# Edge sums of a graph kernel: a 16-column one-hot per tile as stationary operand, in partition quarters, placed by a second product

## What is computed

```python
e   = relu(bn(edge_attr @ ee_w1 + ee_b1, ee_g1, ee_bb1)) @ ee_w2 + ee_b2     # 212500 x 16 -> 128
h   = x + segment_sum(e, dst, N)
z   = h + segment_sum(h[src], dst, N)
z   = relu(bn(z @ mlp_w1 + mlp_b1, ...)); z = relu(bn(z @ mlp_w2 + mlp_b2, ...))
out = layernorm(x + z)
```

## Time and profile before

| | |
|---|---|
| median of three runs | 2196.79 us |
| profiled execution | 2194.66 us |
| its span | 2192.5 us |
| granted TensorE clock, mean over the span | 0.978 |
| PE, DVE, POOL, ACT busy, share of the span | 95%, 78%, 73%, 48% |

### The profile page before, as it was taken

One profiled execution on the slowest core, in us unless ns is written; L12 is line 12 of the kernel. 1 busy time (PEld: TensorE's weight loads), 2 busy tenths in 40 slices (PEclk: granted clock), 3 DMA queues, 4 the chain that ended last, 5 costly groups with the idle time before them and its releaser, 6 DMA issues. The chain is left out here.

```text
span 2192.5 us, 53444 instructions
## 1 busy us (share of the span) xinstructions
PE 2086.0 (95%) x16230; PEld 1694.0 (77%) x16230; DVE 1707.0 (78%) x2494; ACT 1051.6 (48%) x1986; POOL 1601.1 (73%) x1595
## 2 busy tenths in 40 slices
PE   6699999999984999999999999999999999999977
PEld 6699999999952777777777777777777777777637
DVE  5399999999997777777777777777777777777566
ACT  0022222222244555555555555555555555555576
POOL 3288888888868777777777777777777777777405
PEclk8799999999996999999999999999999999999999
DMA  9433333333343211111111111111111111111106
GB/s 212 132 106 105 105 103 104 102 104 104 105 151 126 54 54 53 53 53 53 53 53 53 53 53 53 53 53 53 53 53 53 53 53 53 52 53 54 32 25 210
DMA packets 108752, 169.88 MB, mean 77 GB/s; under 512 B 36800, under 2 KB 65104, under 8 KB 108666
## 3 DMA queue, kind: packets, MB, share of 16 engines
q1 hardware_dynamic: 69213, 96.46, 15.3%
q0 software_dynamic: 34944, 71.64, 11.8%
q10 hardware_dynamic: 4561, 1.36, 0.3%
HBM read 156.54 MB, written 12.81 MB: 77 GB/s over the span
## 5 line engine op out<-in xcount | busy, mean ns | idle before, releaser
L814 POOL DMA_INDIRECT table<-h_scratch,idx x1092 | 1031.1, 944 | 338.0 <-issue 320.9
L946 DVE TENSOR_TENSOR table<-ps,keys 128x880 bf16<-128x880 f32 (+1 forms) x780 | 777.4, 997 | 204.9 <-PE ps L836 193.9
L836 PE MATMUL ps<-table 128*128 128x220 bf16 x2860 | 527.8, 259 | 23.8 <-DVE table L946 23.7
L902 ACT CAST counts_even<-ps 128x440 bf16<-128x440 f32 (+1 forms) x780 | 397.7, 510 | 312.5 <-PE ps L836 291.4
L849 PE MATMUL ps<-table,counts_even 128*128 128x384 bf16 x2600 | 541.7, 326 | 0.0
L849 PE MATMUL ps<-table 128*128 128x384 bf16 x2600 | 538.8, 325 | 0.0
L902 ACT CAST table<-ps 128x440 bf16<-128x440 f32 (+1 forms) x780 | 388.1, 498 | 286.2 <-PE ps L836 261.5
L836 PEld LDWEIGHTS ps<-table 128*128 128x128 bf16 x2860 | 282.7, 101 | 184.0 <-DVE table L946 25.0
L587 PE MATMUL ps<-table 128*128 128x96 f32 x3328 | 415.6, 278 | 0.0
L587 PEld LDWEIGHTS ps<-table 128*128 128x128 f32 x3328 | 389.6, 193 | 0.0
L529 ACT ACTIVATE table<-table,low_rows_sb 128x512 fp32r<-128x512 f32 x208 | 145.0, 720 | 385.4 <-DMA table<-in_edges_t 364.5
(11 more groups left out here) (156 smaller groups left out, 1267.8 us busy)
## 6 DMA issues: line engine op xcount, KB each, us to landing
table<-in_edges_t SPq DMA_DIRECT2D x416, 128.0 KB, 2.5
table<-h_scratch,idx POOLq DMA_INDIRECT x1092, 2.5
table<-in_edges SPq DMA_DIRECT2D x26, 512.0 KB, 7.1
table<-in_x_t SPq DMA_DIRECT2D x48, 256.0 KB, 3.1
h_scratch<-table SPq DMA_DIRECT2D x24, 256.0 KB, 2.2
out<-table SPq DMA_DIRECT2D x24, 256.0 KB, 2.9
table<-in_dst_mixed SPq DMA_DIRECT2D x1, 832.0 KB
table<-in_dst_tiles SPq DMA_DIRECT2D x1, 832.0 KB, 12.5
```

What stands on the lines that cost most here:

```text
L814: pool.indirect_dma_start(near_rows[:, t, :], None, h_dram, bass.IndirectOffsetOnAxis(ap=idx[:, v, t:t + 1], axis=0)).then_inc(gathered[u] ...
L836: mm = pe.matmul(ps[:, LIST_BANKS[p % RING], (t % 2) * LIST_COLS:(t % 2 + 1) * LIST_COLS], low_match[:, v, t, :], match[:, t, :], start=Tr ...
L902: act.copy(counts[(v * LISTS + c) % 2][:, :, 2 * k * NARROW:(2 * k + tiles) * NARROW].rearrange("p b (t w) -> p b t w", t=tiles), ps[:, LI ...
L946: dve.tensor_tensor(match[:, first:last, :], ps[:, 0, 0:LIST_COLS].unsqueeze(1).broadcast_to([P, last - first, LIST_COLS]), keys[:, v, c, ...
```

## The change

The one-hot of a tile becomes 16 columns wide, counted from the first node of that tile (`tile_base`), and is now the stationary operand. The moving operand is the 128 rectified features of the tile with a column of ones behind them (129 columns), so that sums and count come out of one f32 product per tile. Tiles 0 to 3 of a group write the PSUM partition quarters 0 to 3 (16 rows in each), tiles 4 to 7 the same quarters beside them. A second product then puts these rows at their nodes: DVE makes `group_placing`, a one-hot of 2 times 96 columns per group (`place_groups`), ACT copies the sums and the counts out of PSUM (`keep_sums`), and PE multiplies them (`fold_tiles`: two bf16 and two f32 products of 96 columns). `halve` and the counts' four products fall away, and so does the copy of the node numbers in PSUM: `make_onehot` and `place_groups` read `iota` in SBUF. `add_window` comes one group later.

The condition for a single round now also asks that each tile spans under 16 nodes.

```diff
         def window_sums(dve):
-            nodes = ps[:, 5, 0:WINDOW]
+            nodes = iota[:, 0:SLIM]
             def make_onehot(g, u):
                 wait(dve, sums_done, g - 1)
-                dve.tensor_tensor(onehot[:, u % 2], nodes... [P, GROUP_TILES, WINDOW], rel..., ALU.is_equal)
+                dve.tensor_tensor(slim_onehot[:, u % 2], nodes... [P, GROUP_TILES, SLIM], rel..., ALU.is_equal)
             def clamp(g, u):
...
-                dve.tensor_tensor(rows[:, u % 2, :].rearrange("p (t d) -> p t d", d=D),
+                dve.tensor_tensor(edge_rows[:, u % 2, :, 0:D],
...
+            def place_groups(g, u):
+                wait(dve, folded, g - 1)
+                dve.tensor_tensor(group_placing[:, u % 2],
+                                  iota.unsqueeze(1).broadcast_to([P, GROUP_SETS, WINDOW]),
+                                  group_place[:, bass.ds(g * GROUP_SETS, GROUP_SETS)].unsqueeze(2)
+                                  .broadcast_to([P, GROUP_SETS, WINDOW]), ALU.is_equal).then_inc(placed, 1)
...
                         make_onehot(i * BODY + u + 1, u + 1)
                         clamp(i * BODY + u + 1, u + 1)
-                    add_window(i * BODY + u, u)
+                    place_groups(i * BODY + u, u)
+                    if not (first and u == 0):
+                        add_window(i * BODY + u - 1, u - 1)
...
                 @block.scalar
+                    def keep_sums(g, u):
+                        act.wait_ge(sums_done, g + 1)
+                        wait(act, folded, g - 1)
+                        act.copy(tile_counts[:, u % 2], sums_bank(u)[:, :, D:].broadcast_to([P, GROUP_SETS, P]))
+                        act.copy(tile_sums[:, u % 2], sums_bank(u)[:, :, 0:D]).then_inc(sums_kept, 1)
+                    def body(i, last=False):
                         for u in range(BODY):
-                            high(i, u)
+                            if u < 2:
+                                high(i, u + 2)
+                            elif not last:
+                                high(i + 1, u - 2)
+                            keep_sums(i * BODY + u, u)
...
                 @block.gpsimd
-                            halve(i, u)
...
                 @block.tensor
                     def sums(g, u):
-                        wait(pe, added, g - 1)
+                        wait(pe, sums_kept, g - 1)
                         pe.wait_ge(onehot_done, g + 1)
-                        pe.wait_ge(halved, g + 1)
-                        for t in range(GROUP_TILES // 2):
-                            pe.matmul(ps[:, 4 + 2 * (u % 2), WINDOW:2 * WINDOW], ones_bf[:], halves[:, u % 2, t, :], ...)
                         pe.wait_ge(clamped, g + 1)
                         for t in range(GROUP_TILES):
-                            mm = pe.matmul(ps[:, 4 + 2 * (u % 2), 0:WINDOW], rows[:, u % 2, t * D:(t + 1) * D],
-                                           onehot[:, u % 2, t, :], start=(t == 0), stop=(t == GROUP_TILES - 1))
+                            q = t % QUARTERS
+                            mm = pe.matmul(sums_bank(u)[32 * q:32 * q + SLIM, t // QUARTERS, :], slim_onehot[:, u % 2, t, :],
+                                           edge_rows[:, u % 2, t, :], start=True, stop=True, tile_position=(0, 32 * q))
                         mm.then_inc(sums_done, 1)
+                    def fold_tiles(g, u):
+                        wait(pe, added, g - 1)
+                        pe.wait_ge(sums_kept, g + 1)
+                        pe.wait_ge(placed, g + 1)
+                        for k in range(GROUP_SETS):
+                            pe.matmul(folded_at(u)[:, 1, :], tile_counts[:, u % 2, k, :],
+                                      group_placing[:, u % 2, k, :].bitcast(BF16)[:, 1:2 * WINDOW:2], ...)
+                        for k in range(GROUP_SETS):
+                            mm = pe.matmul(folded_at(u)[:, 0, :], tile_sums[:, u % 2, k, :], group_placing[:, u % 2, k, :], ...)
+                        mm.then_inc(folded, 1)
...
                                 features(g + 1, u + 1)
                             sums(g, u)
+                            if not (first and u == 0):
+                                fold_tiles(g - 1, u - 1)
```

More of the change, by code:

```diff
@@ L37 @@
 WINDOW = 96
+SLIM = 16
+QUARTERS = 4
 NEAR = 64
@@ L125, in build @@
         block_mask = carve(0, P)
-        dst_i = carve(0, ALL_TILES).bitcast(I32)
+        tile_base = carve(0, ALL_TILES)
+        dst_i = tile_base.bitcast(I32)
+        group_place = carve(0, GROUPS * GROUP_SETS)
         ones = carve(0, P)
@@ L171, in build @@
         prod = sb("prod", [ED, 2, D])
[L172 to L175, removed]
+        least = sb("least", [MIXED, ROW_ENDS])
+        most = sb("most", [MIXED, ROW_ENDS])
+        turned_ends = sb("turned_ends", [MIXED, QUARTERS, MIXED_TILES // QUARTERS])
         base = sb("base", [P, BASES])
@@ L267, in _ @@
-                act.wait_ge(base_out, 16 * (4 + DENSE))
+                                  least[:, GATHER_AT[-1] + t:GATHER_AT[-1] + t + 1]).then_inc(base_out, 16)
+                act.wait_ge(base_out, 16 * (6 + DENSE))
                 act.dma_start(base[:], base_dram.rearrange("(o g) -> o g", o=1).broadcast_to([P, BASES])
                               ).then_inc(base_in, 16)
-                act.wait_ge(ones_set, 2)
+                act.wait_ge(ones_set, 3)
+                for q in range(QUARTERS):
+                    act.dma_start(group_place[32 * q:32 * q + SLIM, :],
+                                  quarters_dram[q:q + 1, :].broadcast_to([SLIM, GROUPS * GROUP_SETS])).then_inc(place_in, 16)
@@ L339, in _ @@
                 mixed = table[0:MIXED, 1, 0:MIXED_EDGES].bitcast(I32)
[L340 to L345, removed]
+                for k, (op, far) in enumerate(((ALU.min, least), (ALU.max, most))):
+                    dve.tensor_reduce(far[:, 0:MIXED_TILES], mixed.rearrange("r (t e) -> r t e", e=P), AX_X, op
                                       ).then_inc(ends, 1)
                     dve.wait_ge(ends, k + 1)
-                    dve.tensor_reduce(far[:, STREAMS + DENSE:], far[:, STREAMS:STREAMS + DENSE], AX_X, op
+                    at = MIXED_TILES
+                    dve.tensor_reduce(far[:, at:at + ROW_GROUPS],
+                                      far[:, 0:MIXED_TILES].rearrange("r (j t) -> r j t", j=ROW_GROUPS), AX_X, op)
+                    at += ROW_GROUPS
+                    for j in range(STREAMS):
+                        dve.tensor_reduce(far[:, at + j:at + j + 1], far[:, GATHER_AT[j]:GATHER_AT[j + 1]], AX_X, op)
+                    at += STREAMS
+                    if k == 0:
+                        dve.tensor_copy(turned_ends[:], far[:, 0:MIXED_TILES].rearrange("r (i q) -> r q i", q=QUARTERS))
+                    dve.tensor_reduce(far[:, at:at + 1], far[:, GATHER_AT[-1]:MIXED_TILES], AX_X, op
                                       ).then_inc(base_ready, 1)
@@ L491, in body @@
                         clamp(i * BODY + u + 1, u + 1)
-                    add_window(i * BODY + u, u)
+                    place_groups(i * BODY + u, u)
+                    if not (first and u == 0):
+                        add_window(i * BODY + u - 1, u - 1)
+            dve.memset(edge_rows[:, :, :, D:], 1.0)
+            for u in range(2):
+                dve.memset(sums_bank(u), 0.0)
             make_onehot(0, 0)
             clamp(0, 0)
-            body(0)
+            body(0, first=True)
             with dve.Fori(1, BODIES - 1) as i:
@@ L530, in high @@
                                        ACT.Copy, scale=low_rows[:, 0:1]).then_inc(high_done, 1)
-                    for u in range(BODY):
-                        high(0, u)
-                    with act.Fori(1, BODIES) as i:
-                        for u in range(BODY):
-                            high(i, u)
+                    def keep_sums(g, u):
[4 more added lines that the diff above has]
+                    def body(i, last=False):
+                        for u in range(BODY):
+                            if u < 2:
[3 more added lines that the diff above has]
+                            keep_sums(i * BODY + u, u)
+                    high(0, 0)
+                    high(0, 1)
+                    body(0)
+                    with act.Fori(1, BODIES - 1) as i:
+                        body(i)
+                    body(BODIES - 1, last=True)
                 @block.gpsimd
```

134 lines of the change are left out of this document (77 added, 57 removed).

## The result

The changed kernel takes 2221.88 us (median of four runs, 2218.34 to 2224.34) against 2197.28 for the kernel before, a ratio of 1.0111 with a 95% interval of 1.0093 to 1.0128: 1.1% slower, clear of no change. The profiled execution took 2218.34 us with a span of 2216.5, so the comparison with the profile before is +24.0 us of span.

The account below looks back on a forecast made before the run. PE was full before; with the change, DVE and POOL blocking at SBUF was to bound. 208 x (2.8 - 2.528) = +56.6, +4, +1 on 2194.66, runs 2.1 above: 2258 us, range 2130 to 2343, the case's own 2217 to 2311.

Parts of the forecast that it names:

- the period of 2.8 us: Edge stage: time per group with the change, taken at 2.8 us against 2.528 before, +56.6 us over 208 groups.
- DVE's own sum: Edge stage: DVE's work per group, 2.05 us against 2.52 before, including 0.16 of issue behind add_window.
- PE's sums: Edge stage: 16 instructions of 129 moving columns per group, taken at 1.0 us between bounds of 0.45 and 1.79.
- the period of 2.7 to 3.0: Edge stage: sign of being right, 2.7 to 3.0 us per group with PE idle before sums and fold_tiles.
- The blocking term: Edge stage: DVE operations with two SBUF inputs and POOL's split wait for each other, at least 0.6 us per group.
- the two orders of `split` and the placing operation: Edge stage: placing operation first gives 2.73 us per group, split first gives 2.99.
- the prediction's own formula: Edge stage, split first: period P is 2.05 + (2.7 - P + 1.28) - 0.06, so 2.99 us.
- The cost of the change of width: PE running empty between full width and quarters, twice per group: 0 to 0.28 us each, taken at 0.15.
- Prologue and tail: Added DVE operations and later Gram loads before the edge stage, +4 us; one more keep_sums, fold_tiles and addition after, +1.
- Rival 2: Edge stage: f32 products on quarters don't overlap, PE bounds at 3.2 us per group, 2341 us; chance 14%.
- rival 1: Edge stage: split falls under the clamp, so the kernel is faster, 2176 us, other end 2123; chance 30%.
- Rival 3: Edge stage: four quarters fully side by side, sums at 0.45 us, 2239 us if SBUF waits hold; chance 15%.

Follow-up runs that it names:

- Experiments 1 and 2: Kernel before, make_onehot reading iota in SBUF: 2329.81 us. Changed kernel, node numbers in PSUM for both operations, only placing, only one-hot: 2103.98, 2103.57, 2104.05 us.
- both_psum: Changed kernel with make_onehot and place_groups reading node numbers from PSUM and the placed sums sharing one bank: 2103.98 us, ratio 0.9566.
- one_fold_bank: Changed kernel with the placed sums in one PSUM bank instead of two, all node numbers still in SBUF: 2222.28 us, ratio 1.0107.
- pad_act: Changed kernel with one more ACT copy of 256 elements per group, its result unused: 2246.81, 2248.93, 2250.66 and 2131.14 us.
- place_psum: Changed kernel with only place_groups reading node numbers from PSUM and the placed sums sharing one bank: 2103.57 us, one run at 2172.6.
- place_first: Changed kernel with the placing operation ahead of the clamp on DVE: 2195.43 us, ratio 0.9981.
- experiment 3: The run one_fold_bank: changed kernel with the placed sums in one PSUM bank instead of two, 2222.28 us.
- experiment 7: ACT's high one group earlier, ahead of keep_sums: on both_psum 2072.42 us, on the changed kernel 2222.34 us.

## Why the prediction came out as it did

The direction and the mechanism were right, the size was not: +61 us forecast, +24.6 measured. The step that failed is the period of 2.8 us, for which 2.614 was measured: 208 x 0.186 is the 39 us too much. Its two terms that were mis-sized are DVE's own sum and PE's sums. The time lies in the stated range of 2217 to 2311, near its lower end, but the period of 2.7 to 3.0, named as a sign of being right, did not come.

- **The blocking term was right in kind.** The prediction asked for a placing operation or one-hot far above 0.3 us. It is 1.043. The sum of the three means is 0.33 + 1.04 + 1.28, 0.73 above 0.29 + 0.355 + 1.28, where at least 0.6 was named. Experiments 1 and 2 show the cause.
- **The period was taken at 2.8 and is 2.61.** It was chosen between 2.73 and 2.99, the two orders of `split` and the placing operation, and both were too long. *DVE's sum of 2.05*: I counted in every group the 0.16 of issue that the earlier trace rows show behind one `add_window`. In the trace before, only 49 of 206 groups have it, all of them groups in which DVE had just waited for PE. The last groups of the stage have no `split` beside them and show DVE's own pace, 645.25 - 643.39 = 1.86:

```profile
643.39 0.34 DVE L525 TENSOR_TENSOR table<-summed,table 128x192 f32<-128x192 f32 x1
...
643.65 0.34 DVE L520 TENSOR_TENSOR table<-table,ps 128x192 f32 x1
...
643.92 0.28 DVE L500 TENSOR_TENSOR table<-summed,rel 128x128 f32<-128x128 f32 x1
644.12 1.21 DVE L510 TENSOR_TENSOR table<-ps,ee_negshift 128x1024 f32<-128x1024 f32 x1
...
645.25 0.34 DVE L525 TENSOR_TENSOR table<-summed,table 128x192 f32<-128x192 f32 x1
```

- *The sums at 1.0*: they take some 0.4 (four fours at 0.11, and 16 x 0.024 by the starts), the lower bound of 0.45 and not the middle. My reason for the middle (only the next product's first instruction can run beside a product's second) is not borne out, as the starts come in fours. So `split` was ready 302.88 - 300.63 = 2.25 us after a clamp's end and not 2.7. With both terms put right the prediction's own formula gives (2.25 + 1.87 + 1.28 - 0.06)/2 = 2.67, 2% above the measured 2.61 (2.63 in the groups where the blocking holds, see below). With the 2.05 alone put right and 2.7 kept it would have given 2.90.
- **The cost of the change of width was about right.** From `features` to the sums and from the sums to the counts the timeline of `both_psum` has 0.66 and 0.57 us. Less 0.56 and 0.4, that leaves 0.27 for two changes, where 0.3 was taken.
- **Prologue and tail.** +4 was forecast and +4.6 came: PE ended its Gram products' long run 3.1 us later (76.13 against 73.03 for the instruction behind them). DVE, which waits for that, went on 2.9 later (76.45 against 73.56) and needed 1.9 more up to the Gram result (82.12 - 76.45 = 5.67 against 77.33 - 73.56 = 3.77). The tail, taken at 1, costs next to nothing: from the last clamp's end to the last addition's end it is 2.7 before and 2.8 with the change.
- **Rivals.** Rival 2 (no overlap) was priced at 2341, and the kernel that makes it true runs at 2311. The lower end of rival 1 was put at 2123. Its own period of 2.05 gives 2196.79 - 0.478 x 208 + 5 = 2102, and `both_psum`, which has that period, runs at 2104. Rival 3's overlap on four quarters is what happened. The Trainium skill (TensorE: Matmul & The Clock Gate, Measured speedup vs the span model) was nearer than my middle value; with its 4 ns I would have taken the lower bound and 2239. The trace has 5 to 20 ns within a four. By their times rival 1 did not hold in any of the eight runs of the changed kernel and of `one_fold_bank`, and `pad_act` fell into it once in four.
- **Rival 1 held at first.** From the second clamp (104.38) to the tenth (121.66) the changed kernel has a period of 2.16, and then it tips:

```profile
121.64 0.72 ACT L578 ACTIVATE table<-table,low_rows_sb 128x512 fp32r<-128x512 f32 x1 [0.84 <-DMA table<-in_edges_t]
121.66 1.22 DVE L510 TENSOR_TENSOR table<-ps,ee_negshift 128x1024 f32<-128x1024 f32 x1
...
122.44 2.62 POOL L607 TENSOR_TENSOR ea_parts<-table 128x512 fp32r<-128x512 f32 x2 [1.90 <-ACT table L578]
...
122.79 1.14 DVE L525 TENSOR_TENSOR table<-summed,table 128x192 f32<-128x192 f32 x1
...
125.14 1.21 DVE L510 TENSOR_TENSOR table<-ps,ee_negshift 128x1024 f32<-128x1024 f32 x1
```

  A load of edge attributes comes late, `high` waits 0.84 for it, two `split` run back to back over the placing operation and the next one-hot, and the next clamp starts 3.48 us later. From there on the period is 2.63. The traces of `one_fold_bank` and `pad_act` tip at the same group, with `high` 1.09 and 0.68 late. `both_psum` and `place_psum` have such a late load too (0.89 and 1.03) and keep 2.04 and 2.05.
- **Still open:** whether the late load is the cause. No run was made with earlier loads, and `place_first` is blocked from its third group on, though no `high` of it waits for a load from 104 to 180 us. Why the same program lands at either level in different runs is open with it.

## What to carry to other kernels

When a VectorE operation with one input in PSUM gets both inputs in SBUF, and GpSimd reads SBUF in the same loop, price the GpSimd instruction's whole duration as a possible wait in each group: here it turned a gain of 96 us (`both_psum`, 2104 against 2200) into a loss of 25. Keeping a small constant in a PSUM bank can be worth more than double buffering in that bank, which was worth nothing here (experiment 3). And once no engine is full, look for the ring that closes over two groups; here `high` behind `keep_sums` in ScalarE's order cost 32 us (experiment 7).

## What was not expected of the hardware

- Eight f32 products with 16 stationary columns and 129 moving ones, on four partition quarters in turn, run as four fours, one every 0.11 us, where a single instruction takes 0.11 in one quarter: a factor of 4. (0.024 against 0.111 would be 4.6, but the 15 steps between 16 starts hold only three of the long ones.) ACT begins on the result 0.76 us after the first start (301.53 - 300.77).
- One program can run at two levels by the way in which two engines settle against one another: `pad_act` at 2131 and 2247 to 2251, `place_psum` at 2103 and 2173.
- In the prologue of the changed kernel POOL's scaling of 1664 elements (L615) took 4.47 us, 2.7 ns an element. It is hidden by the first loads of the edge attributes. The first one-hot, issued beside it at 96.47, took 2.78 us and ended at 99.25, 0.95 ahead of POOL's end at 100.20. So a blocked DVE operation does not always wait for the end that the profile shows for POOL's.
